# Scores buffer in halves, three of four fill copies on ScalarE, and the expert-weight cuts spread over three stages

## Chip, cores and metric
The kernel runs on one core of a Trainium2 chip. The metric is the device time of one execution in microseconds (us): the median of the runs given below.

## What is computed
x is 16 x 256 x 256 (batches, positions, channels). Four sublayers follow each other, each with a residual:

```python
x = x + L0_xattn(ctx, ctx, layernorm(x), mask, W_out, b_out)   # 16 heads of 16; softmax(where(mask == 0, -1e20, q k^T) / 16) v
x = x + L0_ffn(layernorm(x), w1, b1, w2, b2)                   # uint8 activations, int8 weights, relu, 256 -> 1024 -> 256
x = x + L1_xattn(layernorm(x), ctx, ctx, Wq, ..., Wo, bo)      # autocorrelation by FFT, top 6 lags, weighted rolls of v
x = x + L1_ffn(layernorm(x), Wfc_s, ..., Wproj, bproj)         # one shared expert and 8 routed ones, top 2 per row, gelu
```

The change touches the first three. In the first, q is the normalised x and k and v are the context itself, with no projection ahead of them.

## The kernel before
Four functions run one after the other, each in a block of its own; a block begins on every engine when all engines have ended the one before: `attention` (L115), `quant_mlp` (L840), `autocorrelation` (L1256), `moe` (L1608). Each engine has its own queue, whose order is written out by hand, and semaphores join the queues.

**Attention.** PHASES is -2 to 16. Phase B takes eight head pairs hp of three batches at different steps: scores and row maxima of batch B+1; transposed scores, exponentials and weighing of v for batch B; the rest of batch B-1 (back to rows, division, projection, add to X); and the fill of q and k for batch B+2. Precision is kept by splitting q and k into fp16 parts. Banks: `psum_s` (banks 0) holds the scores of one head pair, both heads; `psum_t` (banks 1 and 2) holds transposed scores, two pairs in turn; `psum_o` and `psum_m` are the halves of banks 3 and each serves one small step after another.

- TensorE, `scores` (L504): four matmuls of 48 rows into `psum_s`, after it has waited that VectorE has taken the maxima of the head pair before (`s_red`). `scoresT` (L520) and `scoresT_mask` (L533) write `psum_t`. Then come the small steps, at most two per head pair: `fill` (L469, 8 transposes into `psum_m`, four fills a batch: two for k, two for q), `max_back` (L481), `mask_back` (L492), `weigh` (L545), `out_back` (L560), `out_turn` (L566), `project` (L574, two a batch).
- VectorE, `take_max` (L737): four operations L745 per head pair, one wait for all; `fill` (L728) copies fills 1 and 3; `split_max` (L749) writes the maxima as fp16 parts of q; `see_mask` (L705) at hp 0 of phase b-2, `set_mask` (L712) at hp 1; `normalise` (L760), `add` (L771, two a batch, the second one phase later); `see_rows` (L108) and `see_weights` (L777) prepare the MLP in phases 15 and 16.
- ScalarE: `exponent` (L400) once per head pair, then the copies that belong to it: `fill` (L391) for fills 0 and 2, `copy_max`, `copy_mask`, `copy_out`, `copy_oT`, and `normal_rows` (L382), which writes `q_rows`.
- GpSimd (POOL), L358 to L373: `split_k`, half a cut, `split_q`, `values`, `add_bias`, the other half of the cut. `cut` (L344) is work for the last sublayer: a weight matrix of an expert (a "half" of an expert, 1 MB; 18 halves) is multiplied by 256 and split into two fp16 parts in four pieces of three instructions each (L352, L354, L356).
- SP issues the loads: context, mask and one half per batch, and the store of the cut half to DRAM (`moe_halves`). All 18 halves are loaded, cut and stored in this block.

**MLP.** VectorE first has chains of small operations (L1134 to L1181), joined by two reductions over partitions on GpSimd (L969, L971). GpSimd does nothing else here after setting constants; SP loads the weights of the third sublayer.

**Autocorrelation.** SP loads the context again (L1359 to L1368), first thing in the block; TensorE transposes and projects it, one batch after the other. GpSimd adds a bias to X (L1390) as rows become ready, and waits for ScalarE's `c_xr`.

Of the kernel before, what the change touches and what calls it, by code (L numbers as in the profile page):

```python
# [50 lines left out]
WSCALE = 256.0  # L51

# [61 lines left out]

def attention(nc, d, g, X, ident, banks, halves_dram):  # L115
# [11 lines left out]
    PIECES = 4  # L127
    GROUPS = ((0, NQ), (NQ, 4 * NQ), (4 * NQ, NT))

    with ExitStack() as ctx:  # L130
# [38 lines left out]
        NE, _, F = d["L1_ffn_Wfc"].shape  # L169
        HALF = D * F // P  # L170
        w_in = [sb(f"w_in{s}", [P, HALF]) for s in range(2)]
        w_cut = [sb(f"w_cut{s}", [P, 2, HALF], F16) for s in range(2)]

# [36 lines left out]
        s_wi = [sem(f"moe_half_in{s}") for s in range(2)]  # L210
        s_wc = sem("moe_half_cut")
        s_ws = [sem(f"moe_half_stored{s}") for s in range(2)]

# [14 lines left out]
        PHASES = range(-2, NB + 1)  # L228
        LN_BEGIN, LN_END = 6, 6
# [7 lines left out]
        def _(sp):  # L237
# [10 lines left out]
            def load_half(n):  # L248
                e, s = n // 2, n % 2
                if n >= 2:  # L250
                    sp.wait_ge(s_wc, 3 * PIECES * (n - 1))
                if e == NE:
                    src = (d["L1_ffn_Wfc_s"].rearrange("(k p) f -> p k f", p=P) if s == 0 else
                           d["L1_ffn_Wproj_s"].rearrange("(j p) c -> p j c", p=P))
                else:
                    src = (d["L1_ffn_Wfc"][e].rearrange("(k p) f -> p k f", p=P) if s == 0 else
                           d["L1_ffn_Wproj"][e].rearrange("(j p) c -> p j c", p=P))
                sp.dma_start(w_in[s][:].rearrange("p (k f) -> p k f", k=src.shape[1]), src).then_inc(s_wi[s], 16)

            def store_half(n):  # L260
                sp.wait_ge(s_wc, 3 * PIECES * (n + 1))
                sp.dma_start(halves_dram[n], w_cut[n % 2][:].rearrange("p a n -> p (a n)")).then_inc(s_ws[n % 2], 16)

# [13 lines left out]

            for b in range(NB):
# [11 lines left out]
            for n in range(NB, 2 * (NE + 1)):  # L290
                load_half(n)
                store_half(n - 2)
            for n in range(2 * NE, 2 * (NE + 1)):
                store_half(n)
            for s in range(2):
                sp.wait_ge(s_ws[s], 16 * (NE + 1))

        @block.gpsimd
        def _(pool):
# [44 lines left out]
            def cut(n, lo, hi):  # L344
                s = n % 2
                pool.wait_ge(s_wi[s], 16 * (n // 2 + 1))
                if n >= 2:
                    pool.wait_ge(s_ws[s], 16 * (n // 2))
                for i in range(lo, hi):
                    cols = slice(i * HALF // PIECES, (i + 1) * HALF // PIECES)  # L350
                    done = 3 * (PIECES * n + i)
                    pool.tensor_scalar(w_in[s][:, cols], w_in[s][:, cols], WSCALE, None, ALU.mult).then_inc(s_wc, 1)  # L352
                    pool.wait_ge(s_wc, done + 1)
                    pool.tensor_copy(w_cut[s][:, 0, cols], w_in[s][:, cols]).then_inc(s_wc, 1)  # L354
                    pool.wait_ge(s_wc, done + 2)
                    pool.tensor_tensor(w_cut[s][:, 1, cols], w_in[s][:, cols], w_cut[s][:, 0, cols], ALU.subtract).then_inc(s_wc, 1)  # L356

            for B in PHASES:  # L358
                if real(B + 2):
                    split_k(B + 2)  # L360
                if B >= -1:
                    cut(B + 1, 0, PIECES // 2)
# [9 lines left out]
                if B >= -1:  # L372
                    cut(B + 1, PIECES // 2, PIECES)  # L373

        @block.scalar
        def _(act):
# [14 lines left out]
            def fill(b, f):  # L391
                act.wait_ge(s_fillT, 4 * b + f + 1)
                if f == 0 and b >= 3:
                    act.wait_ge(s_ST, HP * (b - 2))
                if f == 2 and b >= 2:
                    act.wait_ge(s_S, HP * (b - 1))
                dst = kT[b % 3] if f == 0 else qT[b % 2]
                act.activation(dst[:, :, 0:P], psum_m.bitcast(F16).rearrange("p (h q) -> p h q", h=HP), ACT.Copy).then_inc(s_fillA, 1)
# [27 lines left out]
            def copy_oT(b):  # L426
                act.wait_ge(s_oTp, b + 1)
                if b >= 1:
                    act.wait_ge(s_op, NQ * b)
# [3 lines left out]
            for B in PHASES:  # L433
# [5 lines left out]
                for hp in range(HP):  # L439
                    if real(B):  # L440
# [3 lines left out]
                    if hp == 0 and real(B - 1):  # L444
                        copy_out(B - 1, 3)
                    if hp == 1 and real(B + 1):
                        copy_mask(B + 1)
                    if hp == 1 and real(B + 2):
                        normal_rows(B + 2)
                    if hp in (2, 4) and real(B):  # L450
                        copy_out(B, hp // 2 - 1)
                    if hp == 3 and real(B + 2):
                        fill(B + 2, 0)
                    if hp == 3 and real(B - 1):
                        copy_oT(B - 1)
# [1886 lines left out]
```

## Time and profile before
| | us |
|---|---|
| median of 3 runs | 1400.29 (1398.33 to 1403.54) |
| the profiled execution | 1391.09 |
| its span, first to last instruction | 1389.3 |
| busy: TensorE, VectorE, ScalarE, GpSimd | 1225.5, 908.9, 628.3, 576.5 |
| mean granted TensorE clock | 0.966 of full |

The profile shows one execution. Attention runs to about 393.5 us, the MLP to 530.8, the autocorrelation to 719.7, the experts to the end. In the lists PE is TensorE, DVE VectorE, ACT ScalarE, POOL GpSimd, SPq the queue of SyncE; L745 is a line of the kernel. A share of busy time is a mean over stages, so each stage is read by itself.

### The profile page before, as it was taken

How to read it: one execution, taken by the hardware profiler on the slowest of the kernel's cores; microseconds unless marked ns; L12 is line 12 of the kernel's file. 1: busy time of each engine (PE TensorE's matmuls, PEld its weight loads, DVE VectorE, ACT ScalarE, POOL GpSimd, SP SyncE). 2: the span in 40 equal slices, each digit the busy share in tenths (PEclk: the TensorE clock that was granted, in tenths of full speed). 3: DMA queues.
4: the chain of work that ended last, by engine and by line, in shares of the span. 5: the costliest groups of instructions: out<-in, count | busy, mean ns of one | idle time of the engine just before them, and what ended most of it. 6: DMA issues, size and time to landing. Idle time of an engine off the chain costs nothing. (4 is left out here: it accounts for less than half of the span.)

```text
span 1389.3 us, 29923 instructions
## 1 busy us (share of the span) xinstructions
PE 1225.5 (88%) x10852; PEld 940.3 (68%) x10852; DVE 908.9 (65%) x2674; ACT 628.3 (45%) x1081; POOL 576.5 (41%) x604
## 2 busy tenths in 40 slices
PE   3699999999847798997579999897999999999996
PEld 1355555555423366886467988776999998999995
DVE  7898898898869773225456577444666566665663
ACT  2577777777555571334216633222333333333331
POOL 6899999999900000003200004661333333333333
PEclk9999999999959999999898999999999999999999
DMA  6344344245220001110329205326888877888781
GB/s 225 98 147 138 95 147 141 94 144 190 100 91 0 1 1 46 45 30 1 100 84 255 58 1 183 112 89 214 262 249 250 262 242 248 250 250 257 244 244 65
DMA packets 104193, 196.40 MB, mean 141 GB/s; under 512 B 15632, under 2 KB 86928, under 8 KB 91552
## 3 DMA queue, kind: packets, MB, share of 16 engines
q1 hardware_dynamic: 89792, 178.21, 39.9%
q0 software_dynamic: 14304, 16.93, 5.7%
q8 instruction: 57, 0.93, 0.3%
q14 instruction: 40, 0.33, 0.1%
HBM read 144.70 MB, written 52.23 MB: 142 GB/s over the span
## 5 line engine op out<-in xcount | busy, mean ns | idle before, releaser
L1992 PE MATMUL banks<-moe_w,moe_hT 128*128 128x256 f16 x2640 | 300.6, 273 | 7.2 <-issue 7.1
L1992 PEld LDWEIGHTS banks<-moe_w,moe_hT 128*128 128x128 f16 x2640 | 258.8, 98 | 40.5 <-issue 9.9
L1903 ACT ACTIVATE moe_hf<-banks,moe_b 128x256 f32<-128x256 f32 x440 | 184.9, 472 | 182.7 <-PE banks L1979 148.7
L1847 POOL DMA_INDIRECT out_x<-moe_y,slot_owner x78 | 122.0, 1565 | 285.4 <-DVE moe_y L2225 255.9
L1979 PE MATMUL banks<-moe_rT,moe_w 128*128 128x256 f16 x1872 | 211.8, 273 | 0.0
L745 DVE CUSTOM_DVE_ANT_0 masked<-banks,mask_bias 128x256 f32<-128x256 f32 x512 | 185.8, 418 | 22.6 <-PE banks L515 21.9
L1979 PEld LDWEIGHTS banks<-moe_rT,moe_w 128*128 128x128 f16 x1872 | 183.8, 98 | 21.3
L405 ACT ACTIVATE probsT<-banks 128x1024 f32<-128x1024 f32 x128 | 131.3, 1026 | 64.2 <-PE banks L541 64.1
L2112 DVE TENSOR_TENSOR moe_hT<-moe_hf,moe_hT 128x512 f16<-128x512 f32 x220 | 153.6, 698 | 7.6
L2110 DVE CAST moe_hT<-moe_hf 128x512 f16<-128x512 f32 x220 | 95.2, 433 | 64.1 <-ACT moe_hf L1903 43.9
L1833 POOL DMA_INDIRECT slots_x<-moe_xn,pos x64 | 65.0, 1015 | 153.4 <-DVE pos L2176 123.3
L2220 DVE SCALAR_TENSOR_TENSOR moe_y<-banks,moe_b 128x512 f32<-128x512 f32 x39 | 27.0, 692 | 133.5 <-PE banks L1992 133.5
L1887 ACT ACTIVATE moe_rT<-banks 128x512 f16<-128x512 f32 x39 | 23.3, 597 | 195.3 <-PE banks L1964 195.3
L352 POOL TENSOR_SCALAR w_in<-w_in 128x512 f32<-128x512 f32 x72 | 110.2, 1530 | 0.0
L1979 PE MATMUL banks<-moe_xnT,moe_w 128*128 128x256 f16 x768 | 91.3, 277 | 0.0
L356 POOL TENSOR_TENSOR w_cut<-w_in,w_cut 128x512 f16<-128x512 f32 x72 | 83.5, 1160 | 6.2
L1979 PEld LDWEIGHTS banks<-moe_xnT,moe_w 128*128 128x128 f16 x768 | 76.5, 100 | 9.5
L556 PE MATMUL banks<-probsT,v_ones 128*32 128x256 f32 x1024 | 70.2, 393 | 11.0 <-DVE X L775 10.9
L1069 PE MATMUL banks<-xqT,w1T 128*128 128x512 bf16 x256 | 66.3, 389 | 11.7 <-DVE hidden_max L1195 5.4
L515 PE MATMUL banks<-kT,qT 48*128 48x256 f16 x512 | 52.8, 286 | 26.2 <-DVE row_max L745 20.2
L1393 POOL TENSOR_TENSOR X<-X,bias_bc 128x256 f32 x32 | 22.6, 729 | 116.2 <-issue 115.1
L515 PEld LDWEIGHTS banks<-kT,qT 48*128 48x128 f16 x512 | 15.3, 95 | 71.0 <-DVE row_max L745 44.9
(323 smaller groups left out, 2006.7 us busy)
## 6 DMA issues: line engine op xcount, KB each, us to landing
moe_w<-moe_halves SPq DMA_DIRECT2D x80, 1024.0 KB, 5.0
moe_halves<-w_cut SPq DMA_DIRECT2D x18, 1024.0 KB, 8.6
slots_x<-empty_row SPq DMA_DIRECT2D x1, 10140.0 KB, 48.8
moe_rows<-slots_x SPq DMA_DIRECT2D x39, 260.0 KB, 5.8
w_in<-in_L_ffn_Wfc SPq DMA_DIRECT2D x8, 1024.0 KB, 6.3
w_in<-in_L_ffn_Wproj SPq DMA_DIRECT2D x8, 1024.0 KB, 6.5
moe_b<-in_L_ffn_bproj SPq DMA_DIRECT2D x39, 128.0 KB
ctx_rows<-in_ctx SPq DMA_DIRECT2D x16, 256.0 KB, 2.8
```

Source lines behind the costliest of these rows:

```text
L352: pool.tensor_scalar(w_in[s][:, cols], w_in[s][:, cols], WSCALE, None, ALU.mult).then_inc(s_wc, 1)
L356: pool.tensor_tensor(w_cut[s][:, 1, cols], w_in[s][:, cols], w_cut[s][:, 0, cols], ALU.subtract).then_inc(s_wc, 1)
L405: act.activation(probsT[n % EXPS][:].rearrange("p j k q -> p (j k q)"), psum_t[n % 2][:], ACT.Exp, scale=SCALE).then_inc(s_exp, 1)
L515: ins = pe.matmul(psum_s[:, at:at + S], qT[b % 2][rows, hp, t * P:(t + 1) * P], kT[b % 3][rows, hp, :], start=(t == 0), stop=(t == NQ - 1))
L556: ins = pe.matmul(psum_o[i * VW:(i + 1) * VW, 0:S], v_ones[b % 2][:, k, 4 * quad + i, :], probsT[n % EXPS][:, i % 2, k, :], start=(k == 0) ...
L745: ins = v.tensor_tensor_reduce(masked[2 * j + t][:], psum_s[:, at:at + S], mask_bias[b % 2][:, t, :], 1.0, -3e38, ALU.add, ALU.max, row_ma ...
L1847: pool.indirect_dma_start(out=out_rows, out_offset=bass.IndirectOffsetOnAxis(ap=owner[:, s, t:t + 1], axis=0), in_=y[s % 2][:, t, :], in_o ...
L1903: ins = act.activation(hf[p][:, j, :], src, ACT.Gelu_apprx_tanh, bias=b1[buffer][:, j:j + 1], scale=1.0 / WSCALE)
L1979: ins = pe.matmul(banks[jp // 2][:, at:at + SLOT], w1[buffer][:, w, k, j * P:(j + 1) * P], moving(x, k), start=(k == 0 and (w, x) == PARTS ...
L1992: ins = pe.matmul(OUT[p][:, t * D:(t + 1) * D], hT[p][:, x, j, t * P:(t + 1) * P], w2[buffer][:, w, j, :], start=(j == 0 and (w, x) == PAR ...
L2110: v.tensor_copy(hT[p][:, 0, at, :], hf[p][:, at, :]).then_inc(e_hh, 1)
L2112: v.tensor_tensor(hT[p][:, 1, at, :], hf[p][:, at, :], hT[p][:, 0, at, :], ALU.subtract).then_inc(e_hl, 1)
```

## The change
- `psum_s` is handed over in halves. `scores` writes one head of the pair (j), waits only for that head's maxima, and its matmuls alternate with those of `scoresT` for the other head; the small steps on `psum_o` now stand between the two halves, those on `psum_m` after the mask. `take_max` takes one head at a time, with VectorE's other work between.
- Fill 0 goes through `psum_o` at hp 0 and is copied by VectorE; fills 1 to 3 go through `psum_m` at hp 3 to 5 and are copied by ScalarE. `max_back` of the first half moves from hp 5 to hp 6.
- `project` and `add` are one each per batch, at hp 6 of the next phase; the second add no longer stands in the phase after. `see_mask` is taken a phase earlier, at hp 5; `set_mask` is parted into `set_live` and `set_mask`. ScalarE's copies from `psum_o` stand ahead of the exponential of their head pair.
- GpSimd cuts two pieces a phase instead of four, and splits k for batch B+3 at the end of phase B. 9 halves are cut beside attention, 2 in the MLP's block (two pieces before the first reduction over partitions, six after it), 7 in the autocorrelation's block ahead of the bias adds. SP's loads and stores follow; in the autocorrelation they begin before the first context load. `mixT` takes the memory of `zf`.

The diff, cut to its core (moved code that does not change is left out):

```diff
+def load_half(sp, d, w, n):
+    src = expert_half(d, n)
+    if n >= 2:
+        sp.wait_ge(w["cut"], 3 * PIECES * (n - 1))
+    sp.dma_start(w["rows"][n % 2][:].rearrange("p (k f) -> p k f", k=src.shape[1]), src).then_inc(w["in"][n % 2], 16)
+def store_half(sp, w, halves_dram, n):
+    sp.wait_ge(w["cut"], 3 * PIECES * (n + 1))
+    sp.dma_start(halves_dram[n], w["parts"][n % 2][:].rearrange("p a n -> p (a n)")).then_inc(w["stored"][n % 2], 16)
...
@@ attention, SP @@
             for b in range(NB):
                 if b >= 2:
                     load_ctx(b)
                     load_mask(b)
-                load_half(b)
-                if b >= 2:
-                    store_half(b - 2)
+                if b < 2:
+                    load_half(sp, d, w, b)
+                elif b % 2 and (b + 1) // 2 < CUT_BESIDE_ATTENTION:
+                    load_half(sp, d, w, (b + 1) // 2)
+                    store_half(sp, w, halves_dram, (b + 1) // 2 - 2)
...
@@ attention, GpSimd @@
+            split_k(0)
             for B in PHASES:
-                if real(B + 2):
-                    split_k(B + 2)
                 if B >= -1:
-                    cut(B + 1, 0, PIECES // 2)
+                    cut_piece(pool, g.cut, 2 * (B + 1))
...
                 if B >= -1:
-                    cut(B + 1, PIECES // 2, PIECES)
+                    cut_piece(pool, g.cut, 2 * (B + 1) + 1)
+                if real(B + 3):
+                    split_k(B + 3)
...
@@ attention, TensorE @@
+            def scores(b, hp, j, t):
...
+                if n >= 1 and t == 0:
+                    pe.wait_ge(s_red, 2 * (n - 1) + j + 1)
...
+            def both_scores(B, hp, j):
+                for i in range(NQ):
+                    if real(B + 1):
+                        scores(B + 1, hp, j, i)
+                    if real(B):
+                        scoresT(B, hp, 1 - j, i)
...
             for B in PHASES:
                 for hp in range(HP):
+                    both_scores(B, hp, 0)
+                    if hp == 0 and real(B + 2):
...
+                        fill(B + 2, 0)
+                    if hp == 1 and real(B - 1):
+                        if real(B + 2):
+                            pe.wait_ge(s_fillV, (B + 2) + 1)
+                        weigh(B - 1, 3)
...
+                    both_scores(B, hp, 1)
+                    if real(B):
+                        scoresT_mask(B, hp)
...
                     if hp == 4 and real(B + 2):
-                        pe.wait_ge(s_fillA, 2 * (B + 2) + 1)
-                        fill(B + 2, 1)
+                        pe.wait_ge(s_fillA, 3 * (B + 2) + 1)
+                        fill(B + 2, 2)
+                    if hp == 5 and real(B + 2):
+                        pe.wait_ge(s_fillA, 3 * (B + 2) + 2)
+                        fill(B + 2, 3)
...
@@ attention, VectorE @@
+                    if real(B + 1):
+                        take_max(B + 1, hp, 0)
+                    if hp == 0 and real(B + 2):
+                        fill(B + 2)
                     if hp == 1 and real(B + 2):
-                        set_mask(B + 2)
+                        set_live(B + 2)
...
+                    if hp == 5 and real(B + 3):
+                        see_mask(B + 3)
                     if hp == 6 and real(B - 1):
-                        add(B - 1, 0)
-                    if hp == 0 and real(B - 2):
-                        add(B - 2, 1)
+                        add(B - 1)
...
+                        take_max(B + 1, hp, 1)
+                    if hp == 1 and real(B + 2):
+                        set_mask(B + 2)
...
@@ MLP, SP and GpSimd @@
+            for n in range(CUT_BESIDE_ATTENTION + 1, CUT_BESIDE_ATTENTION + CUT_BESIDE_MLP + 1):
+                load_half(sp, d, g.cut, n)
+                store_half(sp, g.cut, halves_dram, n - 2)
...
+            for q in range(AHEAD):
+                cut_piece(pool, g.cut, first + q)
             pool.wait_ge(m_pm, 1)
             pool.partition_all_reduce(all_max[:], part_max[:], P, bass.bass_isa.ReduceOp.max).then_inc(m_am, 1)
+            pool.wait_ge(m_am, 1)
+            for q in range(AHEAD, PIECES * CUT_BESIDE_MLP):
+                cut_piece(pool, g.cut, first + q)
...
@@ autocorrelation, SP and GpSimd @@
+            load_half(sp, d, g.cut, n + 1)
+            store_half(sp, g.cut, halves_dram, n - 1)
+            for b in range(NB):
+                load(b, b % 2)
+                if b in (5, 7, 9, 11, 14):
+                    load_half(sp, d, g.cut, n + 2)
+                    store_half(sp, g.cut, halves_dram, n)
+                    n += 1
...
+            for q in range(PIECES * (CUT_BESIDE_ATTENTION + CUT_BESIDE_MLP), 2 * PIECES * (d["L1_ffn_Wfc"].shape[0] + 1)):
+                cut_piece(pool, g.cut, q)
             pool.wait_ge(c_wr, 4)
```

## Rows read from the trace of the kernel before
**Rows 1.** Stretch of 13 phases: length, busy us of each engine (instructions), clock, DMA.
```profile
68.90:341.60 272.70, 254.83 (x3120) 144.55 (x3120) 242.06 (x1080) 202.43 (x261) 254.67 (x273) 1.00 0.42 133
```
**Rows 2.** Timeline of GpSimd: start, duration, line, operation, [idle before, releaser].
```profile
139.49 0.61 POOL L327 CAST q_split<-q_rows 128x512 f16<-128x512 f32 x1 [0.19 <-ACT q_rows L387]
...
147.18 1.49 POOL L352 TENSOR_SCALAR w_in<-w_in 128x512 f32<-128x512 f32 x1
...
150.54 0.61 POOL L316 CAST k_split<-ctx_rows 128x512 f16<-128x512 f32 x1
```
**Rows 3.** Timeline of TensorE over one phase and into the next.
```profile
160.68 1.07 PE L556 MATMUL banks<-probsT,v_ones 128*32 128x256 f32 x16
161.69 0.39 PE L515 MATMUL banks<-kT,qT 48*128 48x256 f16 x4
161.91 0.38 PE L530 MATMUL banks<-qmT,kT 64*128 64x256 f16 x4
162.23 0.41 PE L541 MATMUL banks<-mask_biasT,ident_b 64*64 64x512 bf16 x4
162.57 0.62 PE L477 MATMUL banks<-ident,k_split 128*128 128x128 f16 x8
163.03 0.61 PE L571 MATMUL banks<-ident,o_rows 128*128 128x128 f32 x4
...
175.71 1.07 PE L556 MATMUL banks<-probsT,v_ones 128*32 128x256 f32 x16 [0.57 <-DVE X L775]
...
177.98 0.23 PE L496 MATMUL banks<-ident_b,mask_bias 128*128 128x128 bf16 x1
...
179.33 0.66 PE L563 MATMUL banks<-ident,oT_raw 128*128 128x128 f32 x4
180.37 0.39 PE L515 MATMUL banks<-kT,qT 48*128 48x256 f16 x4 [0.38 <-DVE row_max L745]
```
**Rows 4.** Timeline of TensorE and VectorE: a projection, and the attention's end.
```profile
167.58 1.08 PE L579 MATMUL banks<-woT,oT 128*128 128x256 f32 x4
...
377.40 2.28 DVE L780 TENSOR_REDUCE sw<-w 128x2 f32<-128x2048 f32 x1
...
380.06 1.93 PE L556 MATMUL banks<-probsT,v_ones 128*32 128x256 f32 x16 [3.68 <-DVE X L775]
```
**Rows 5.** Timeline of VectorE in phases 5 and 6.
```profile
156.25 0.16 DVE L716 TENSOR_SCALAR row_live<-row_top 128x2 f32<-128x2 f32 x1
...
165.45 0.41 DVE L745 CUSTOM_DVE_ANT_0 masked<-banks,mask_bias 128x256 f32<-128x256 f32 x1
165.79 0.68 DVE L735 COPY kT<-banks 128x1024 f16<-128x1024 f16 x1
...
173.78 0.55 DVE L757 SCALAR_TENSOR_TENSOR q_split<-row_max,q_split 128x16 f16<-128x16 f32 x1
...
176.95 0.95 DVE L716 TENSOR_SCALAR row_live<-row_top 128x2 f32<-128x2 f32 x1
```
**Rows 6.** Groups of ScalarE, four phases: count, busy us, mean ns, idle before.
```profile
L398 ACT ACTIVATE kT<-banks 128x1024 f16<-128x1024 f16 x4 | 4.1, 1016 | 0.0
```
**Rows 7.** DMA issues of the 13 phases: count, size, median us to landing.
```profile
moe_halves<-w_cut SPq DMA_DIRECT2D x13, 1024.0 KB, 8.6
...
mask_int<-in_mask_Bx1xSxS_ik SPq DMA_DIRECT2D x12, 256.0 KB, 3.1
```
**Rows 8.** Timeline of VectorE and GpSimd: a norm chain beside cuts, one without, a reduction.
```profile
44.16 0.55 DVE L688 TENSOR_TENSOR nmr<-stats 128x24 f32<-128x24 f32 x1
...
400.98 0.22 DVE L1147 TENSOR_TENSOR nmr<-stats 128x32 f32<-128x32 f32 x1
...
405.69 1.23 POOL L969 PARTITION_ALL_REDUCE all_max<-part_max  x1 [10.27 <-DVE part_max L1164]
```
**Rows 9.** Timeline where the autocorrelation begins: first context loads, first transposes.
```profile
530.86 78.38 SPq L1362 DMA_DIRECT2D c_rows<-in_ctx  x16
...
538.73 1.35 PE L1464 MATMUL banks<-flip,c_rows 128*128 128x128 f32 x8 [2.10 <-DVE bias_bc L1540]
```

More of the change, by code:

```diff
@@ L51 @@
 WSCALE = 256.0
+PIECES = 4
+CUT_BESIDE_ATTENTION = 9
+CUT_BESIDE_MLP = 2
 def ln_memory(ctx, nc, NT):
@@ L439, in _ @@
                 for hp in range(HP):
+                    if hp == 1 and real(B - 1):
+                        copy_out(B - 1, 3)
+                    if hp == 2 and real(B + 1):
+                        copy_mask(B + 1)
+                    if hp in (3, 5, 7) and real(B):
+                        copy_out(B, hp // 2 - 1)
+                    if hp == 4 and real(B - 1):
+                        copy_oT(B - 1)
                     if real(B):
@@ new lines, in _ @@
+                    if hp == 4 and real(B - 1):
+                        pe.wait_ge(s_ov, 4 * B + (1 if real(B) else 0))
+                        out_turn(B - 1)
+                    if hp == 5 and real(B):
+                        if real(B - 1):
+                            pe.wait_ge(s_oT, B)
+                        weigh(B, 1)
+                    if hp == 6 and real(B - 1):
+                        if real(B):
+                            pe.wait_ge(s_ov, 4 * B + 2)
+                        project(B - 1)
@@ L788, in _ @@
             norm_begin(0)
+            see_mask(0)
+            norm_end(0)
             for B in PHASES:
@@ L823, in _ @@
                         norm_begin(1)
-                    if hp == 7 and real(B + 2):
-                        fill(B + 2, 3)
                     if B == -1:
@@ L1362, in load @@
                 sp.dma_start(ctx_in[s][:], rows[:, b, :, :]).then_inc(c_ctx[s], 16)
-            for b in range(2):
-                load(b, b)
-            with sp.Fori(1, NB // 2) as i:
-                for s in range(2):
-                    load(2 * i + s, s)
+            n, halves = CUT_BESIDE_ATTENTION + CUT_BESIDE_MLP, 2 * (d["L1_ffn_Wfc"].shape[0] + 1)
+            load_half(sp, d, g.cut, n + 1)
[6 more added lines that the diff above has]
+                    n += 1
+            assert n == halves - 2
+            for n in range(halves - 2, halves):
+                store_half(sp, g.cut, halves_dram, n)
+            for s in range(2):
+                sp.wait_ge(g.cut["stored"][s], 16 * (halves // 2))
             sp.wait_ge(c_lw, 2)
@@ L2259, in program @@
                                     dft_flipped=[P, g.NQ, g.S], idft=[P, 3, g.S], dc=[P, 1])
+                half = g.D * F // P
+                g.cut = {
+                    "rows": [to_lag.enter_context(nc.sbuf_tensor(f"half_rows{s}", [P, half], F32)) for s in range(2)],
+                    "parts": [to_lag.enter_context(nc.sbuf_tensor(f"half_parts{s}", [P, 2, half], F16)) for s in range(2)],
+                    "in": [to_lag.enter_context(nc.semaphore(f"half_in{s}")) for s in range(2)],
+                    "cut": to_lag.enter_context(nc.semaphore("half_cut")),
+                    "stored": [to_lag.enter_context(nc.semaphore(f"half_stored{s}")) for s in range(2)],
+                }
                 with ExitStack() as to_mlp:
```

299 lines of the change are left out of this document (117 added, 182 removed).

## Prediction
> **What bounds the kernel now.** I read the views in this order. The stretches by stage first [rows 1]: from 68.90 to 341.60 us lie 13 equal phases of the attention, 272.70 / 13 = 20.98 us each, with TensorE busy 254.83 / 13 = 19.60 us of each, GpSimd 19.59, VectorE 18.62 and ScalarE 15.57, at a granted clock of 1.00 (2.4 GHz). Three engines are nearly full, so the waits decide. GpSimd is not the pacer: it starts each query split only when ScalarE has delivered q_rows [rows 2], and nothing in the phase waits for it. TensorE waits for VectorE: 0.57 us for an addition before weigh, then up to 0.38 us for the row maxima before scores [rows 3]. This is the ping-pong over one scores buffer, worst where VectorE has most queued (the end of one phase and the first two head pairs of the next).
>
> Next I price what TensorE must stream in a phase, from start to start [rows 3]. Scores 0.22, transposed scores 0.32 and mask 0.34 give 0.88 per head pair, 7.0 for eight. Four weighings cost 1.01 each (4.0), four fills 0.46 (1.8), two max_back the same (0.9), mask_back 1.35, two out_back and out_turn about 0.6 each (1.8), the projection 2 x 1.0 (busy 1.08 each [rows 4], less the overlap that the other groups show, 0.07). The sum is 19.0 us. The phase takes 21.0, so 2.0 us are stalls.
>
> **The change part by part, attention.** I walk one steady phase in the new order, head pairs hp0 to hp7, time 0 at hp0 on TensorE. Half a row-max pass costs VectorE 0.7 us: two operations, each 165.79 - 165.45 = 0.34 from start to start [rows 5].
> (a) GpSimd loses two of four cut pieces. One piece takes 150.54 - 147.18 = 3.36 us [rows 2], so its load falls from 19.6 to 12.9 us, and it stands idle from before hp0 until q_rows comes (end of hp1, about 6 us). VectorE's small operations in that time run free: row_live takes 0.16 us free and 0.95 beside GpSimd; the second operation of split_max, of like size, takes 0.55 beside it [rows 5], so I put it at 0.2 free. I take 0.45 us off split_max's two and 0.6 off set_live.
> (b) hp7 to hp0. The last scores half starts at -0.6, its maxima end at 0.5, split_max 0.95, half a pass 1.65, the VectorE fill (0.68) 2.35. TensorE is ready for weigh at 2.1 and waits 0.3 for that fill. That wait is new: behind it stand hp1's second scores half and all after it.
> (c) hp1 to hp2: mask_back and out_back are covered, VectorE is done with normalise at 6.7, TensorE comes at 6.9. No stall.
> (d) Fill 1, 2 and 3 follow each other through one bank, each released by a ScalarE copy of 1.02 us [rows 6] that stands behind an exponential. At hp4 ScalarE has copy_oT 0.6, exponential 1.03, copy 1.02, so 2.65 us against TensorE's 2.1: stalls of 0.1 before fill 2 and 0.13 before fill 3. ScalarE as a whole goes from 15.6 to 16.6 us of some 19.8, which is covered.
> (e) One add of 512 columns at hp6 (0.6) instead of two of 256; TensorE reaches weigh 0.6 us after it is done. Costs nothing; the old wait of 0.57 goes, and those for row maxima with it, since the next scores half needs only its own half's maxima.
> (f) see_mask(B+3) moves to hp5. Its load is queued on SP behind values(B+1), which ends at about 9.3; issue at 9.7 and landing 3.1 us later [rows 7] give 12.8, and VectorE comes at 13.0. If late, VectorE has until 14.8 before TensorE waits.
> (g) TensorE now switches between packed row groups and full-array groups eight more times in a phase. No row shows such a switch cost apart; neighbouring starts [rows 3] bound it between 0 and the 0.09 by which a transposed pair exceeds a scores pair. Nearest to 0; I take 0.15 us a phase, and 0.7 as the end.
> Sum: 19.0 + 0.5 + 0.15 = 19.7, and 0.1 for what a hand walk misses: 19.8. The gain is 13 x (21.0 - 19.8) = **15.6 us** (ends: 13 x 0.3 = 4 with VectorE's operations as slow as now, 13 x 1.9 = 25 without a stall).
>
> **Around it.** The two phases without a fill or without scores give 0.6 and 0.4: **1.0**. The start up to 68.9 us is VectorE's (scores, statistics and copies back to back): two copies of 0.68 fewer and about 1.1 less contention: **2.5** (0 to 4). The end: TensorE waits 3.68 us before the last weigh for an add that stands behind the 2.28 us weight reductions on VectorE [rows 4]. The new order has no such wait, and one projection and one add instead of two. The reductions are then still ahead of normalise, so I take off the 3.7, and 0.8 for the projection and add that are joined: **4.5** (3 to 6). The stores of the last halves leave this stage too; SP was done before VectorE, so nothing.
>
> **Where the cuts go.** Eight pieces (27 us) go beside the MLP. Two run before the first reduction over partitions, 6.8 us from 395.4, done by 402.2; the reduction started at 405.69 [rows 8]. It is covered by 3.5 us. Six follow it, 20 us, until about 428, beside the scale chain and the first rounding steps. The cost is VectorE's: an operation of the layer-norm chain takes 0.55 beside GpSimd against 0.22 free [rows 8], and over a six-step chain this makes 0.5 to 0.9 us. Three such chains and four rounding steps: **+3.5** (0.5 to 7).
> The other 28 pieces stand in the autocorrelation: 28 x 3.36 = 94 us from about 533.5, plus some 1 us waiting for a store (8.6 us to land [rows 7]), so done near 629. The bias adds that follow on GpSimd wait for rows that are ready from 640 on, so this is hidden. SP's context loads stand behind waits for cuts: the tightest, half 14, is cut at 588, and load 12 is due at 589.5. Also hidden, with 1.5 us. But the first context load is issued behind a 1 MB load and a 1 MB store: from 530.86 that is 0.4 to the store's issue and 8.6 to its landing [rows 7], and 1.1 for a quarter megabyte at that pace, about 541, while TensorE is ready at 538.73 [rows 9]. **+2** (0 to 4). The Trainium skill, DMA: Bandwidth & Descriptors, section Queues, rings and completion order, has each engine take descriptors in ring order, which is the 2; if the context overtook, it would land about 3 us after its issue and cost nothing. The mix table in the place of zf is loaded after zf's last use: nothing.
>
> **Sum.** 15.6 + 1.0 + 2.5 + 4.5 - 3.5 - 2 = 18.1 us. The profiled execution took 1391.09 us (span 1389.3), so 1373.0 for one like it. The timed runs lie 9.2 us above it; the same gain from their median of 1400.29 gives **1382 us**.
>
> **The rivals.** (A) The stalls move and don't go: ScalarE's copies in a row and the new wait before weigh take what the halves give. With split_max and set_live as slow as now the same walk gives 0.12 + 0.26 + 0.32 + 0.35 + 0.27 + 0.25 = 1.6 us of stalls and a phase of 20.7. For it: GpSimd's place in the phase may drift. Against it: it has 7 us of slack. Then 13 x 0.3 + 1.0 + 2.5 + 4.5 - 5.5 = 6.4, so 1394. Chance 0.24.
> (B) TensorE streams with no stall and the cuts cost VectorE little: 25 + 8 - 3 = 30, so 1370. For it: VectorE keeps 2 us of slack a phase. Chance 0.14.
> (C) Slower: the mask for see_mask comes late. It is issued only after GpSimd's values, in the same phase that needs it. From a landing at 14.8 us on, each microsecond counts in every phase; the 1.2 gained is gone at 16.0, which is 6.3 us after issue, where 3.1 is the median and the halves' 8.6 the far end. At 8 us after issue the phase takes 22.7: 13 x 1.7 = 22 lost, 2.5 gained around it, so 1420. Against it: the half transfers end early in the phase, before this load. Chance 0.06.
> (D) The change doesn't do what it says: the scores halves do nothing, because TensorE's order makes each wait anyway, and the copies on ScalarE cost what VectorE saves: a phase of 21.0; 8 - 5.5 = 2.5 gained, so 1398. Chance 0.06.
> (E) Beside the MLP every small VectorE operation waits for the GpSimd instruction under way, not only the first of a chain: some 16 operations at half a mean GpSimd instruction (3.36 / 3 / 2 = 0.56 us) cost 9 us instead of 3.5, so 1388. For it: row_live at 0.95. Against it: the later steps of a chain beside GpSimd take their free time. Chance 0.06. The Trainium skill, SBUF — State Buffer, section Who interferes with whom, states this for the port pair that the two engines share: whoever comes second blocks for the whole instruction. By that rule it is these 9 us; the rows agree that there is blocking, but not at each step.
>
> **How the numbers follow.** The forecast, 1376 to 1389, has 0.44. The range reaches down to B's middle and up through nearly all of A and D's middle: 1369 to 1398; it leaves out C, the outer half of B and some of D. Some 0.5% (7 us) is what a measurement of this kernel can tell from no change, so faster means under 1393.3. Forecast 0.44, B 0.14, E 0.06 and 0.4 of A (0.10) make faster 0.74; the rest of A and D make the same 0.20; C makes slower 0.06.
>
> **What would show it.** In the profile after: phases of 19.5 to 20.2 us between successive row_live operations, TensorE's share of idle under 1 us a phase, GpSimd idle 6 to 7 us before each q_split cast and row_live at 0.16; a wait of about 0.3 before the fourth weighing on VectorE's fill; no 3.7 us gap before the last weigh; the MLP stretch 2 to 5 us longer and the first context transpose about 2 us late. Phases of 20.7 and waits of TensorE on ScalarE's fills show A, waits of VectorE for mask_int show C. I am wrong in the size if the switches in (g) cost 0.1 us each.

## The result and the profile after

The changed kernel takes **1391.14 us** (median of 5, 1386.98 to 1396.29) where the kernel before, run beside it, takes 1398.58 (1395.14 to 1403.54): a ratio of 0.9951, with an interval of 0.9929 to 0.9974. It gains 7.4 us (4 to 10). The prediction of 1382 us had the sign right and the time in its range of 1369 to 1398, but not in its forecast of 1376 to 1389, and the gain is less than half of the 18 us forecast.

Two single executions mislead here. The profiled one of before (1391.09 us) was that kernel's fastest, and the first one of after (1396.29 us) the slowest of that kernel's five; their spans say "no change". Both kernels were therefore profiled once more, and these executions (1398.10 and 1389.82 us) lie near the medians. The columns before and after are of these second profiles, by stage, in us:

| stage | before | after | difference | forecast | first profiles |
|---|---|---|---|---|---|
| start to the first steady row_live | 72.8 | 74.6 | +1.8 | -2.5 | 72.2, 76.2 |
| a steady phase (13 of them) | 21.01 | 20.27 | 13 x -0.74 = -9.6 | -15.6 | 21.01, 20.27 |
| rest of the attention | 49.3 | 45.1 | -4.2 | -5.5 | 48.6, 44.4 |
| MLP | 138.80 | 141.02 | +2.2 | +3.5 | 137.02, 143.57 |
| autocorrelation | 189.33 | 192.25 | +2.9 | +2 | 188.80, 191.07 |
| experts (unchanged) | 672.87 | 671.55 | -1.3 | 0 | 669.60, 675.63 |
| sum | 1396.2 | 1388.0 | -8.2 | -18.1 | 1389.3, 1394.4 |

The start, the MLP and the experts vary by up to a few us between executions of one kernel; the mean length of a phase doesn't, by more than 0.01 us. The MLP took 140.4 to 144.8 us in the eight profiles in which its code is that of the changed kernel, against 137.0 and 138.8 before, so its loss may well be nearer 5 us than 2.2. Part of this spread goes with the clock: the mean granted clock of the stage was 0.90 in the two shortest of the eight (140.4 and 141.0) and 0.88 to 0.89 in the other six (143 or more); before, it was 0.92 with 137.0 and 0.88 with 138.8. Between executions with like clocks the loss is 3.4 to 6 us.

The stretch from 90 to 310 us, first of after, then of the second profile of before (length, then busy us of PE, PEld, DVE, ACT, POOL, the clock, DMA share and rate). It answers [rows 1]:

```profile
90.00:310.00 220.00, 220.00 (x2621) 114.65 (x2620) 184.66 (x883) 178.22 (x230) 141.94 (x163) 1.00 0.24 76
```
```profile
90.00:310.00 220.00, 204.62 (x2504) 115.79 (x2505) 195.93 (x870) 162.44 (x209) 205.62 (x221) 1.00 0.40 130
```

TensorE is now busy in all 220 us. No wait of it is left: the list of waits of this stretch begins with GpSimd, which stands idle 6.6 us a phase, as step (a) had it, and VectorE's row_live is never slow any more (min/median/max 161/164/167 ns, where [rows 5] had 0.95 us):

```profile
POOL q_split L344 <- ACT q_rows L391: 73.0, 11, 6.6
ACT probsT L409 <- PE banks L549: 31.3, 55, 1.5
DVE masked L747 <- PE banks L518: 24.5, 66, 0.6
```
```profile
L719 DVE TENSOR_SCALAR row_live<-row_top x13: 161/164/167, 76.2 to 319.5; 128x2 f32<-128x2 f32 x13
```

So in the steady phases the stalls went altogether, better than forecast, and the phase is still 0.5 us longer than the 19.8 that I gave it with stalls. What TensorE streams costs 20.27 us, not 19.0. The timeline of TensorE shows where (start, duration, line, operation; L518 is scores, L531 scoresT, L482 a fill, L579 out_turn, L549 the mask):

```profile
142.66 0.41 PE L549 MATMUL banks<-mask_biasT,ident_b 64*64 64x512 bf16 x4
143.00 0.62 PE L482 MATMUL banks<-ident,k_split 128*128 128x128 f16 x8
143.55 0.28 PE L518 MATMUL banks<-kT,qT 48*128 48x256 f16 x1
143.56 0.28 PE L531 MATMUL banks<-qmT,kT 64*128 64x256 f16 x1
143.67 0.27 PE L518 MATMUL banks<-kT,qT 48*128 48x256 f16 x1
143.68 0.27 PE L531 MATMUL banks<-qmT,kT 64*128 64x256 f16 x1
143.88 0.66 PE L579 MATMUL banks<-ident,o_rows 128*128 128x128 f32 x4
144.47 0.28 PE L518 MATMUL banks<-kT,qT 48*128 48x256 f16 x1
```

Read the starts. Two row groups side by side step on after 0.12 us (143.55 to 143.67), but the second step of a half takes 0.20 to 0.21 (143.67 to 143.88), and what follows it has another shape. A half costs 0.32, a head pair 0.64, where 0.22 + 0.32 = 0.54 stood before [rows 3]. And the fill takes 0.55 (143.00 to 143.55), not the 0.46 of [rows 3]: that row was a fill followed by out_turn, which uses the array in the same way. A row of the kernel before that I passed over has the other price already, a fill followed by a weigh, 148.62 to 149.17:

```profile
148.62 0.62 PE L477 MATMUL banks<-ident,q_split 128*128 128x128 f16 x8
149.17 1.07 PE L556 MATMUL banks<-probsT,v_ones 128*32 128x256 f32 x16
```

With these prices the sum is 16 x 0.32 + 8 x 0.34 + 4 x 1.01 + 6 x 0.55 + 1.36 + 3 x 0.59 + 1.92 = 20.2 us: the phase. In the kernel before the same prices give two of the four fills 0.55, so its stream was 19.2 us and its stalls 1.8: the change took 1.8 us of stalls out of a phase and put 1.1 us into the stream. The Trainium skill, TensorEngine Tiling (Array Packing), section Key Properties, says that changing the tiling mode, not only the tile, drains TensorE. The rows agree that a change costs time, 0.08 to 0.1 us where a row with it and one without can be compared; a drain itself they do not show. It bears on step (g), and the prediction did not use it.

### The profile page after: what moved, and what is told of

It reads as the page before. It is cut to its first block and busy times, and to the rows that moved or that the text cites. A ratio compares the mean times of both kernels' runs of the same rounds, so it can differ in the third digit from the quotient of the medians.

```text
span 1394.4 us, 29774 instructions
## 1 busy us (share of the span) xinstructions
PE 1237.5 (89%) x10841; PEld 934.3 (67%) x10852; DVE 882.6 (63%) x2642; ACT 641.1 (46%) x1097; POOL 574.5 (41%) x604
## 5 line engine op out<-in xcount | busy, mean ns | idle before, releaser
L2016 PE MATMUL banks<-moe_w,moe_hT 128*128 128x256 f16 x2640 | 296.9, 273 | 0.0
L747 DVE CUSTOM_DVE_ANT_0 masked<-banks,mask_bias 128x256 f32<-128x256 f32 x512 | 193.2, 420 | 37.4 <-PE banks L518 37.3
L409 ACT ACTIVATE probsT<-banks 128x1024 f32<-128x1024 f32 x128 | 131.1, 1025 | 47.1 <-PE banks L549 45.1
L152 POOL TENSOR_SCALAR half_rows<-half_rows 128x512 f32<-128x512 f32 x72 | 107.6, 1494 | 17.5 <-issue 17.4
L518 PE MATMUL banks<-kT,qT 48*128 48x256 f16 x512 | 103.9, 286 | 10.2 <-DVE row_max L747 8.5
L531 PE MATMUL banks<-qmT,kT 64*128 64x256 f16 x512 | 100.3, 278 | 0.0
L156 POOL TENSOR_TENSOR half_parts<-half_rows,half_parts 128x512 f16<-128x512 f32 x72 | 84.0, 1166 | 6.2
L1081 PE MATMUL banks<-xqT,w1T 128*128 128x512 bf16 x245 | 64.9, 392 | 13.1 <-DVE hidden_max L1207 5.6
L518 PEld LDWEIGHTS banks<-kT,qT 48*128 48x128 f16 x512 | 28.7, 95 | 68.5 <-DVE row_max L747 40.5
```

What stands on the lines that cost most here:

```text
L152: pool.tensor_scalar(rows[:, cols], rows[:, cols], WSCALE, None, ALU.mult).then_inc(w["cut"], 1)
L409: act.activation(probsT[n % EXPS][:].rearrange("p j k q -> p (j k q)"), psum_t[n % 2][:], ACT.Exp, scale=SCALE).then_inc(s_exp, 1)
L518: ins = pe.matmul(psum_s[:, at:at + S], qT[b % 2][rows, hp, t * P:(t + 1) * P], kT[b % 3][rows, hp, :], start=(t == 0), stop=(t == NQ - 1))
L531: pe.matmul(psum_t[n % 2][:, at:at + S], kT[b % 3][rows, hp, k * P:(k + 1) * P], qmT[b % 2][rows, hp, :], start=(k == 0), stop=False)
L747: ins = v.tensor_tensor_reduce(masked[2 * j + t][:], psum_s[:, at:at + S], mask_bias[b % 2][:, t, :], 1.0, -3e38, ALU.add, ALU.max, row_ma ...
L2016: ins = pe.matmul(OUT[p][:, t * D:(t + 1) * D], hT[p][:, x, j, t * P:(t + 1) * P], w2[buffer][:, w, j, :], start=(j == 0 and (w, x) == PAR ...
```

## The experiments

A time without a range is of one execution. The lengths of phases, which the readings rest on, repeat to 0.01 us.

**The changed kernel again** (no edit).

> The changed kernel, unaltered, once more. In the first profile of it the attention ended 9.75 us earlier than in the kernel before, the MLP took 6.5 us longer, the autocorrelation 2.6 and the MoE part 5.8. Theory: the attention (phases of 20.27 us), the MLP's late first reduction (3.7 us) and the late first context load (1.9) are properties of the kernel and come back; the 5.8 us of the MoE part, whose instructions did not change, are variation between executions, so the MoE part comes out anywhere between 669 and 676. Rival: the MoE part is slower because of something the change left behind (rings, addresses); then it is 675 to 677 again. Median against before: 7 us faster by the theory, 0 to 2 by the rival.

Measured: 1390.37 us (1387.57 to 1399.04), ratio 0.9948 (0.9926 to 0.997). Phases of 20.27 us; the MoE part (the experts) 671.55, so the 5.8 us there were variation. The late reduction over partitions and the late context load came back; both are told below.

**The kernel before again** (no edit).

> The kernel before, unaltered, once more, for its stages: its first profile (1391.09 us) was its fastest execution, 7.5 us under the median of the runs then, and stage by stage it stands only 1.3 us above a median profile of the changed kernel, where the medians differ by 7.4. Theory: the fast one had luck in stages that the change doesn't touch (MoE 669.6 us, the rest 671 to 673) and in the MLP (137.0); a usual one has phases of 21.0, MLP 137 to 139, autocorrelation 188.8 to 190 and MoE 671 to 674. Rival: the phases themselves vary, 21.0 to 21.4 us, and the attention's gain is 14 us rather than 10.

Measured: 1398.15 us (1391.8 to 1400.82). Phases of 21.01, MLP 138.80, autocorrelation 189.33, MoE 672.87: the theory. The attention ended 12.0 us later than in the changed kernel's second profile.

**Are the switches the price? Both halves of a head pair back to back, in all head pairs, and in four (JOINED = (3, 4, 5, 6)).**

```diff
+            JOINED = (0, 1, 2, 3, 4, 5, 6, 7)
                     both_scores(B, hp, 0)
+                    if hp in JOINED:
+                        both_scores(B, hp, 1)
...
-                    both_scores(B, hp, 1)
+                    if hp not in JOINED:
+                        both_scores(B, hp, 1)
```

> The two scores halves of every head pair are issued back to back, and the step that stood between them behind them; nothing else changes. Theory (a switch from row-packed matmuls to others costs TensorE 0.08 to 0.1 us): the two halves take 0.54 to 0.56 us from start to next start where they take 2 x 0.32 now, so TensorE's stream falls from 20.27 to about 19.5 us a phase, and waits for row maxima come back, 0.5 to 1.5 us a phase, so phases of 20.0 to 21.0. Rival (the 0.32 is the price of the interleaved order itself, not of the switch): 0.64 stays, and with waits the phase is 20.8 to 21.8.

> As the run before, but only head pairs 3 to 6 have their halves back to back, where VectorE has least queued. Switch theory: 4 x 0.09 = 0.36 us off the stream, no or short new waits, so phases of 19.9 to 20.1 and 3 to 5 us less in all than the changed kernel. Rival (waits eat it): phases of 20.3 or more, no gain.

Measured: all eight, 1404.53 us, phases of 21.40, more than the theory's 21.0. Four, 1399.67 us (1394.55 to 1402.25), ratio 1.0009 (0.9989 to 1.0029), phases of 20.86. TensorE's timeline with four joined:

```profile
187.44 0.28 PE L518 MATMUL banks<-kT,qT 48*128 48x256 f16 x1
187.44 0.28 PE L531 MATMUL banks<-qmT,kT 64*128 64x256 f16 x1
187.56 0.27 PE L518 MATMUL banks<-kT,qT 48*128 48x256 f16 x1
187.56 0.38 PE L531 MATMUL banks<-qmT,kT 64*128 64x256 f16 x2
187.67 0.27 PE L518 MATMUL banks<-kT,qT 48*128 48x256 f16 x1
187.78 0.27 PE L531 MATMUL banks<-qmT,kT 64*128 64x256 f16 x1
187.78 0.27 PE L518 MATMUL banks<-kT,qT 48*128 48x256 f16 x1
187.98 0.66 PE L579 MATMUL banks<-ident,o_rows 128*128 128x128 f32 x4
...
193.11 0.28 PE L518 MATMUL banks<-kT,qT 48*128 48x256 f16 x1 [0.73 <-DVE row_max L751]
```

Two halves take 187.44 to 187.98 = 0.54 us, with the same matmuls in the same alternating order: the last step alone has the extra. TensorE's queue has a wait for s_red between the two halves also here, and the step over it takes no more than 0.11 us, so the wait instruction isn't the price either. It belongs to the change of shape, and not to the order within the halves. That a smaller stream makes a shorter phase is refuted, and of my expectation for four only its rival held: the wait of 0.73 us at head pair 6 comes because VectorE must do four maxima and see_mask (0.98 + 0.69 us) before it hands back the second half. Against all eight joined, the halves buy out nearly 2 us of waits (21.40 less a stream of about 19.5) for 0.8 us of switches.

**Did GpSimd's relief do it? Its work in the attention brought back.**

```diff
     pool.wait_ge(w["cut"], 3 * q + 1)
+    if twice:
+        pool.tensor_copy(parts[:, 0, cols], rows[:, cols]).then_inc(w["again"], 1)
...
+        pool.tensor_tensor(parts[:, 1, cols], rows[:, cols], parts[:, 0, cols], ALU.subtract).then_inc(w["again"], 1)
...
+        pool.tensor_scalar(rows[:, cols], rows[:, cols], 1.0, None, ALU.mult).then_inc(w["again"], 1)
```

> The changed kernel with GpSimd's work in the attention brought back to what it was: each of the two cut pieces of a phase is worked twice (cast, subtraction and a multiplication by 1.0 are repeated on the same columns), so GpSimd is busy some 19.6 us a phase again. Theory (TensorE's own stream of 20.27 us sets the phase, and VectorE has 3 us of slack): phases of 20.3 to 20.5; the halves made the gain. Rival (GpSimd's relief is what took the waits away, as my walk with slow VectorE operations had it): phases of 20.7 to 21.0, with waits of TensorE on VectorE.

Measured: 1403.11 us, phases of 21.20. GpSimd is busy 205.29 of 220 us, as before, and TensorE no longer all of it:

```profile
90.00:310.00 220.00, 212.33 (x2504) 110.00 (x2500) 191.16 (x844) 170.50 (x218) 205.29 (x219) 1.00 0.23 73
```
```profile
178.03 0.33 DVE L764 TENSOR_SCALAR q_split<-row_max 128x16 f16<-128x16 f32 x1
178.40 0.67 DVE L766 SCALAR_TENSOR_TENSOR q_split<-row_max,q_split 128x16 f16<-128x16 f32 x1
```
```profile
180.37 0.42 PE L571 MATMUL banks<-probsT,v_ones 128*32 128x256 f32 x4 [0.21 <-DVE kT L745]
...
185.39 0.66 PE L578 MATMUL banks<-ident,oT_raw 128*128 128x128 f32 x4 [0.36 <-DVE o_rows L777]
```

The expected theory fell and the rival held, with a phase even longer than its 21.0. The second step of the split of the maxima takes 0.67 us beside GpSimd, and the weigh behind VectorE's fill waits, the very place that step (b) named. With GpSimd full the halves are worth less than nothing: 21.20 against 21.01. Without the halves, the relief alone (all eight joined) gives 21.40. Only both together give 20.27. One limit: the joined runs keep the new order of the small steps, so they aren't the kernel before with less GpSimd work.

**Is ScalarE's third copy worth anything? VectorE copies the fourth part again.**

```diff
@@ ScalarE @@
-                    if hp == 5 and real(B + 2):
-                        fill(B + 2, 3)
@@ VectorE @@
+                    if hp == 6 and real(B + 2):
+                        last_fill(B + 2)
```

> The changed kernel, but VectorE copies the fourth filled part again, so two of four are ScalarE's as before the change. Theory (TensorE's stream of 20.27 us sets the phase; VectorE is busy 17.0 us of it, ScalarE 16.4): VectorE rises to 17.7 and has still 2.5 us, so phases of 20.3 to 20.6. Rival (VectorE is where the waits are made, so each 0.7 us counts): 20.8 or more, with waits of TensorE for row maxima near head pairs 6 to 0.

Measured: 1392.54 us, phases of 20.27, TensorE busy 220.00 of 220, VectorE 190.79 instead of 184.66, ScalarE 169.56 instead of 178.22. The third copy moves load and buys no time.

**The start: the second batch's context split ahead of the bias addition.** TensorE's first fill of batch 1 moved from hp 3 to hp 0, ahead of the second half, and waited there (changed kernel):

```profile
26.47 1.01 PE L482 MATMUL banks<-ident,k_split 128*128 128x128 f16 x8 [5.75 <-POOL k_split L336]
```
```diff
+                if B == -2:
+                    split_k(B + 3)
                 if real(B + 2):
                     add_bias(B + 2)
```

> The changed kernel, but in its first phase GpSimd splits the second batch's context ahead of the bias addition, not behind it. In the changed kernel TensorE's first fill of the second batch stands ahead of the second scores half and waits 5.75 us for that split, which waits for the addition, which waits for the last start-up load (22.6 us). Theory: the wait goes, and the first steady row_live comes 3 to 5 us earlier than 74.6 to 76.2; the attention ends at 379 to 381 instead of 383.2 to 384.1. Rival (the start is VectorE's anyway, so the wait only moves): less than 1 us.

Measured: 1386.84 us. The fill starts at 19.60 us without a wait, the first steady row_live at 69.6, the attention ends at 377.94, 5.2 us sooner than in the changed kernel's second profile. The start varies, so over more profiles (those of the joined halves and of the full GpSimd left out, whose attention runs otherwise): first steady row_live at 72.9 to 76.2 us in six without the edit (mean 74.8) and at 69.6, 70.4 and 72.0 in three with it (mean 70.6), some 4 us.

**The MLP: where the eight pieces stand.** GpSimd in the changed kernel, and with all eight behind the first reduction:

```profile
391.42 1.15 POOL L156 TENSOR_TENSOR half_parts<-half_rows,half_parts 128x512 f16<-128x512 f32 x1
400.72 0.38 POOL L978 PARTITION_ALL_REDUCE all_max<-part_max  x1 [8.15 <-issue]
407.89 1.53 POOL L152 TENSOR_SCALAR half_rows<-half_rows 128x512 f32<-128x512 f32 x1 [6.79 <-issue]
```
```profile
394.91 1.13 POOL L978 PARTITION_ALL_REDUCE all_max<-part_max  x1 [10.36 <-DVE part_max L1176]
403.01 1.53 POOL L152 TENSOR_SCALAR half_rows<-half_rows 128x512 f32<-128x512 f32 x1 [6.96 <-issue]
```
```diff
-            first, AHEAD = PIECES * CUT_BESIDE_ATTENTION, 2
+            first, AHEAD = PIECES * CUT_BESIDE_ATTENTION, 0
```

> The changed kernel, but all eight cut pieces beside the MLP stand behind the first reduction over partitions; before, two stood ahead of it. Theory (GpSimd needs some 7 us between ordinary instructions and the reduction, with nothing recorded, and the two pieces push these 7 us past the moment at which VectorE is ready): the reduction starts within 0.3 us of VectorE's part_max, the MLP takes 3 to 4 us less than the 141.0 to 143.6 of the changed kernel, so 137.5 to 140. Rival (the reduction waited for the ports or for something VectorE does): the gap stays and the MLP takes 141 to 144. Under the theory a gap of 7 us also stays between the reduction and the first piece.

Then all eight behind the second reduction:

```diff
-            pool.wait_ge(m_am, 1)
-            for q in range(AHEAD, PIECES * CUT_BESIDE_MLP):
-                cut_piece(pool, g.cut, first + q)
             pool.wait_ge(m_hp, 1)
             pool.partition_all_reduce(h_all[:], h_part[:], P, bass.bass_isa.ReduceOp.max).then_inc(m_ha, 1)
+            pool.wait_ge(m_ha, 1)
+            for q in range(PIECES * CUT_BESIDE_MLP):
+                cut_piece(pool, g.cut, first + q)
```

> The changed kernel, but all eight pieces stand behind the second reduction, so none runs beside the layer norm, the scale chain or the rounding steps before it. Theory (of the MLP's extra time 3.7 us are the late reduction and the rest VectorE's and the clock's delay beside the pieces): the MLP takes 137 to 138.5 us, as in the kernel before (137.0). Rival (the pieces cost VectorE as much wherever they stand, because its hq steps run beside them now): 140 or more.

Measured: 1389.56 us and an MLP of 139.89; 1385.75 us and 139.91. Starts, counted from the start of the MLP (part_max is VectorE's input to the first reduction, s_in the scale made from its result, hidden_max the first maxima of the hidden layer):

| | part_max | reduction | s_in | first hidden_max | whole |
|---|---|---|---|---|---|
| before, first profile | 11.5 | 11.8 | 13.1 | 21.9 | 137.0 |
| after, first and second | 12.7 | 16.6 | 17.0 | 24.9 | 143.6, 141.0 |
| pieces behind the first reduction | 11.5 | 11.9 | 13.1 | 22.3 | 139.9 |
| pieces behind the second | 11.5 | 11.9 | 13.1 | 22.3 | 139.9 |

Between a cut and the reduction GpSimd has some 8 us in which nothing is recorded, and 7 again between the reduction and the next cut. VectorE is ready at 12.7, 1.2 us late because its layer-norm chain ran beside cuts, and then waits until 16.6 for the reduction to begin. Together s_in is 3.9 us late and the first hidden_max 3.0. With the pieces behind, no gap stands ahead of the reduction and both are back within 0.4. The second reduction starts at 68.7 and 69.7 us before, at 73.2 and 72.8 after, at 70.6 with the pieces behind the first reduction and at 69.2 with all behind the second. So up to there the late pieces lose nothing. Behind it they slow VectorE's hq operations (rounding of the hidden layer), 0.97 us on average for 0.69, and the stage is as long as with the other edit. Of the whole stage the edits take off 1.1 to 3.7 us, but only 0.5 to 1.1 against the two executions of the changed code with a clock of 0.90, which these two have too (0.90 and 0.91). The theory for the late pieces, 137 to 138.5, was too good. The Trainium skill, GPSIMD Engine Reference, section 2.1 Instruction dispatch, says that the first call to freshly loaded code costs some 6 us with no instruction in the profile. Here the gap is 6.7 to 7.5 us from a reduction to a cut in the twelve profiles that have one there, eleven times with the DMA queues idle, and 6.9 to 10.3 from a cut to the reduction in eight, with the DMA engines 71 to 97% busy. That the gap is the loading of code no run shows.

**The autocorrelation: first context loads ahead of the half.**

```diff
+            for b in range(2):
+                load(b, b % 2)
             load_half(sp, d, g.cut, n + 1)
             store_half(sp, g.cut, halves_dram, n - 1)
```

> The changed kernel, but in the autocorrelation the first two context loads are issued ahead of the load and the store of a half (2 MB). Theory (the context waits behind these 2 MB): the first turn of the context starts 7.5 to 8 us after the stage begins, as in the kernel before, instead of 9.75, and the stage takes 1.5 to 2 us less than 191.1 to 192.3. Rival (TensorE is not ready before that in any case, or the cuts that then start later set the end): no difference, 191 or more.

Measured: 1391.64 us; the first turn comes 7.9 us after the stage's start instead of 9.5 to 9.8, so the 2 us of my step are real, at 1.6 to 1.9. But the stage takes 192.99: nothing gained. A gap of GpSimd again is why: its first cut in this stage starts 11.5 us in (10.62 us of idle, behind memsets that run at once), not 2.6 as I had it, so all cuts are 9 us late, and context loads that stand behind a wait for a cut are late in turn. In the profiles it is 10.6 to 12.1 us, longer than the 7 of the MLP; why, these runs don't tell. In the changed kernel:

```profile
539.19 1.53 POOL L152 TENSOR_SCALAR half_rows<-half_rows 128x512 f32<-128x512 f32 x1 [10.62 <-issue]
```
```profile
602.73 0.66 PE L1488 MATMUL banks<-flip,c_rows 128*128 128x128 f32 x4 [1.27 <-DMA c_rows<-in_ctx]
```

With the MLP's pieces behind its second reduction the gap is over before the stage begins, the first cut runs 1.0 us in, no context load but the first is late, and the stage takes 189.7.

**The three edits together.**

> The three edits together: the second context split ahead of the bias addition, the MLP's pieces behind the second reduction, the first two context loads ahead of the half. Theory: the gains add where they lie in different stages: 5.2 us at the start, 2 (1 to 3.5) in the MLP, 1.5 in the autocorrelation since the cuts there begin 10 us earlier, and now also the 1.9 us of the first context load, which alone gave nothing because a later context load waited for a late cut (the context phase grew from 82.6 to 86.2 us). Median near 1380, autocorrelation 187.5 to 188.5. Rival (the first load's gain is lost again in the loop): autocorrelation 189.5 to 190, median 1382.

Measured: **1382.11 us** (1378.23 to 1383.42), ratio 0.9876 (0.9852 to 0.99) to the kernel before: better than both. Attention 379.59, MLP 139.81, autocorrelation 189.07, between theory and rival: the first turn comes at 7.9 us and no context load is late, yet only 0.7 us of the 1.6 remain; which step takes the rest I did not find. The stage is then as short as in the kernel before (188.8 and 189.3), so the cuts there cost nothing any more. The median is the 1382 of the rival. That it is also the 1382 us of the prediction is chance: the prediction was of another kernel.

**A third piece in every fourth phase.**

> The combined kernel with four more pieces beside the attention (every fourth phase cuts three, not two) and four fewer beside the MLP. Theory (GpSimd stands idle 6.7 us a phase, so a third piece of 3.4 us is free as long as it ends before VectorE's small operations): attention as in the combined kernel within 0.5 us, MLP 138 to 139.5 instead of 139.9. Rival (a third piece moves into row_live and the statistics of the row maxima, as four pieces did at 0.9 us a phase): 0.3 to 0.5 us more in each of the four phases, so 1 to 2 us more in the attention, and no gain.

Measured: 1384.43 us (1378.26 to 1386.86), ratio 0.9895 (0.986 to 0.9931). Phases of 20.45 on average, MLP 138.4. Three of the 13 phases have a third piece and cost 0.7 us more each, 2.1 in all, where the rival had 0.3 to 0.5; the MLP gives 1.4 back. No gain, as the rival had it; the two medians differ by less than the executions of either. Idle time of GpSimd isn't free if VectorE's small operations come within it.

## Why the prediction was right and wrong

- **What bounds the kernel** was right: waits between TensorE and VectorE over one buffer, sharpened by GpSimd. The waits of the steady phases are gone.
- **The stream of 19.0 us** was the first step to fail. Four fills and two max_back at 0.46 came from one row, a fill followed by a matmul of the same shape. All six cost 0.55 now, since scores follow each: +0.5 us a phase.
- **(g), the switches.** I took 0.15 us a phase, with 0.7 as the end, "nearest to 0". The halves cost 8 x 0.1 = 0.8. The text said itself that 0.1 a switch would make the size wrong, and it did. Both together are 1.3 us a phase where I had 0.15, and since the 0.5 us of stalls and the 0.1 for a hand walk didn't come, the phase missed by 0.47 us: 6 of the 10 us that the sum is off. That it missed by so little is luck, as two errors of opposite sign met.
- **(a)** was right in mechanism and numbers, and weighed more than I wrote: without it the halves gain nothing. **(b) and (d)** named stalls of 0.3, 0.1 and 0.13 that no phase has. For (b) the trace shows why: VectorE's fill ends 2.32 us after hp0 begins (I had 2.35), but TensorE comes at 2.42, not 2.1, since its stream is longer. **(c) and (e)** held. **(f)** held: no wait for the mask.
- **The start** was mis-signed: I counted VectorE's savings (2.5) and did not walk the first phase with the fill at hp 0. With that wait removed the first steady row_live comes at 70.6 us on average, 1.9 before the 72.5 of the kernel before: most of the forecast term, which that wait (5.75 us, 4.22 in the second profile) had hidden.
- **The end**: the 3.7 us wait is gone, 4.2 of 5.5 us came. The last weigh now waits 1.13 us for the exponential, and the second out_back behind it for rows that stand behind the weight reductions, 1.57 and 1.11 us in the two profiles where it was 0.81. Neither was in my sum; that they make the missing 1.3 us is not tested. The last projection runs at half clock (3.78 us for what takes 1.92 else), but the last two of the kernel before did too (2.07 and 2.08 us).
```profile
372.32 1.07 PE L564 MATMUL banks<-probsT,v_ones 128*32 128x256 f32 x16 [1.13 <-ACT probsT L409]
376.18 0.66 PE L571 MATMUL banks<-ident,oT_raw 128*128 128x128 f32 x4 [1.57 <-DVE o_rows L770]
```
- **The MLP**: 2.2 to 6.5 for 3.5, for another reason. "Covered by 3.5 us" was the failed sentence: the two pieces end early enough (392.6 us), the reduction does not start after them for 8 us.
- **The autocorrelation**: the first load's 2 us measured 1.6 to 1.9. "Hidden, with 1.5 us" failed, by an unrecorded gap of the same kind.
- **Rivals.** A's mechanism, slow operations of VectorE with GpSimd busy, is real but needs GpSimd full. B's premise, no stall at all, was what happened, at another price of the stream. C, D and E did not occur; that the halves do nothing (D) is near the truth only with GpSimd full. That the time lay in the range owes something to chance: the start was 4.3 us worse than forecast and the steady phases 6, while the MLP's other cause happened to cost about its forecast.

## What to carry to other kernels

When a change interleaves matmuls of different tile shapes, count the changes of shape and price each from a pair of rows that has one; take no duration from a row without looking at what follows it. A change in the order of steady work is also to be walked through the first and last rounds, where the inputs of a moved step may not be there. And where GpSimd alternates between ordinary instructions and a reduction over partitions, the unrecorded gap on both sides belongs in the plan: put its spare work where the gap is covered, not where the busy times fit.

## What was new about the hardware

- In the pairs of rows that can be compared here, TensorE adds 0.08 to 0.1 us when the next matmul has another tile shape: 0.12 us from step to step within a half, 0.20 at its end; 0.55 for a fill before scores or weigh, 0.46 before full-array work. Whether it is the array that drains or the next weights that can't be loaded ahead, these runs don't tell.
- GpSimd stands 6.9 to 10.3 us (8.15 in the first profile) between a cut and a reduction over partitions, with nothing recorded, and 6.7 to 7.5 between the reduction and a cut. Where memsets come 70 us after the reduction and a cut behind them, the memsets start at once and the cut 10.6 to 12.1 us later. Where cuts came before the memsets (the late pieces), the next cut starts 1.0 us into the stage.
- Beside full GpSimd work VectorE's operation of 16 columns takes 0.67 us, alone 0.23. Four pieces in a phase of the changed kernel cost 0.9 us, a third one 0.7 in the phase that has it; with two TensorE has no wait.
